# Decoder layer on one core: the 4-bit code lookup of the feed-forward takes its maxima with one four-way reduction for each side of the table

## Chip, core and metric

The kernel runs on one core of one Trainium2 chip. The metric is the device time of one execution, in microseconds (us). The core has five engines that run at the same time: TensorE (PE in the profile, with PEld for the loading of its weights), VectorE (DVE), ScalarE (ACT), GpSimd (POOL) and SyncE (SP), which here only issues DMA transfers. Each engine works through its own instructions in order and waits on semaphores for the others.

## The reference, cut to what matters

A decoder layer on x of 4 x 512 rows and 1024 columns: self-attention, cross-attention, and a feed-forward whose three weight matrices are stored as 4-bit codes with one scale for each block of 64.

```
NF4_CODE = [-1.0, -0.696, -0.525, -0.395, -0.284, -0.185, -0.091, 0.0, 0.080, 0.161, 0.246, 0.338, 0.441, 0.563, 0.723, 1.0]
Wg, Wu, Wd = NF4_CODE[codes] * scale of the block            # each 1024 x 3584 in all
g = x @ Wg.T ;  u = x @ Wu.T ;  h = silu(g) * u ;  x = x + h @ Wd.T
```

The table value of a code is computed without a gather. The table is convex above its zero and concave below. So the value is the maximum of four straight lines of the code (with a zero cut-off in one of them) less the maximum of four others. The change concerns how these two maxima are taken.

## The kernel before, in words

First comes the attention part (until about 946 us of the span), which the change doesn't touch. Then comes `feed_forward`. The hidden size of 3584 is cut into 28 chunks of 128, and two chunks make a group, so there are 14 groups. Group 0 and the last are written out, and those between are a hardware loop. On TensorE a group is `gate_up` for both chunks: eight steps q = 0 to 7, each with 24 gate and 24 up matmuls of 512 columns. Then follows `down`, with 16 row tiles r of 12 matmuls each, which sum into two PSUM buffers in turn. Down of row r waits for `y_added` of row r - 2. A gate or up matmul of step n waits until the PSUM bank of step n - 2 has been read (`silu_done`, `h_done`).

While TensorE works on a group, the other engines make the weights of the tiles to come: 12 tiles of 128 x 512 in a group, numbered k, six of them ahead of the group. For one tile:

- SP loads codes and scales into one of two slots (`codes`, `scales`).
- ACT draws eight lines of the codes (`draw_line`, L1547 for the first two, with Relu, and L1550 for the rest) into the tile `line`. There is one set of eight lines only, so a line is drawn anew when DVE has finished with the old one.
- DVE takes six pairwise maxima (`look_up`, L1625): upper and lower lines alternate, and each result overwrites the next line of its side. A seventh instruction, L1631, writes the difference into `w32` (two buffers).
- POOL multiplies by the scales (`scale`, L1426). ACT rounds to fp16 (`cut_high`, L1555, which comes after the third line of the tile two further on). POOL takes the remainder (`cut_low`, L1431), and `w_low` counts these.

DVE also does `hidden` for each step q (L1661, h = silu(g) * u, from PSUM) and `add_down` for each row r (L1666, adds into y). ACT does `gate_silu` (L1578) and `hidden_high` (L1583), POOL `hidden_low` (L1445). The order on each engine is written out by hand. `CUTS` says which of a group's 84 lookup instructions (7 for each of 12 tiles) DVE issues in which step q; the last 14 are interleaved with `add_down`, one after each row. `FIRST_CUTS` does so for group 0, in which the layer norm is done between the first steps. The lookups of step q come ahead of `hidden(q)`. ACT draws lines one tile ahead of DVE, by the same cuts; `gate_silu(q)` comes after three quarters of the lines of its step, and in the first two steps of group 0 the layer norm's ACT work comes behind them.

Of the kernel before, what the change touches and what calls it, by code (L numbers as in the profile page):

```python
# [8 lines left out]
FP32 = mybir.dt.float32  # L9
# [3 lines left out]
ALU = mybir.AluOpType  # L13
ACT = mybir.ActivationFunctionType
AX_X = mybir.AxisListType.X
# [6 lines left out]
P = 128  # L22
# [8 lines left out]
HALF = 512  # L31
# [17 lines left out]
def code_line(lo, hi):  # L49

    slope = np.float32(F_SCALE * (NF4[hi] - NF4[lo]) / (hi - lo))
    return float(slope), float(np.float32(F_SCALE * NF4[lo] - float(slope) * lo))
# [4 lines left out]
UPPER_LINES = [code_line(8, 9), code_line(10, 11), code_line(12, 13), code_line(14, 15)]  # L57
LOWER_LINES = [tuple(-v for v in code_line(*at)) for at in ((5, 6), (3, 4), (1, 2), (0, 1))]


LINES = [line for pair in zip(UPPER_LINES, LOWER_LINES) for line in pair]
NL = len(LINES)
LUT = 7


class Attention:
# [1187 lines left out]
def feed_forward(nc, dram):  # L1254

    with ExitStack() as ctx:
        def sb(name, shape, dt):
            return ctx.enter_context(nc.sbuf_tensor(name, shape, dt))
# [15 lines left out]
        dn_l = sb("dn_l", [P, 2, C], FP16)  # L1274
        codes = sb("codes", [P, 2, HALF], INT32)
        scales = sb("scales", [P, 2, HALF], FP32)
        line = sb("line", [P, NL, HALF], FP32)
        above = sb("above", [P, 1], FP32)
        below = sb("below", [P, 1], FP32)
        w32 = sb("w32", [P, 2, HALF], FP32)  # L1280
# [16 lines left out]
        consts = sem("consts")  # L1297
# [8 lines left out]
        lined = sem("lined")  # L1306
        lut = sem("lut")
        scaled = sem("scaled")
        w_high = sem("fw_high")
        w_low = sem("fw_low")  # L1310
# [14 lines left out]
        NQ = 2 * NB  # L1325
        AHEAD = 6
# [11 lines left out]
            return (2, (k - 6) // 2, k % 2) if k < 10 else (3, 0, k % 2)  # L1338


        CUTS = [0, 9, 18, 27, 36, 45, 54, 62, 70, 84]
        FIRST_CUTS = [-14, -7, 0, 7, 14, 28, 42, 56, 70, 84]

        def cuts_of(first):
            return FIRST_CUTS if first else CUTS


        def ended_in(q, first):
            lo, hi = cuts_of(first)[q:q + 2]
            return range(lo // LUT, hi // LUT)  # L1350

        def lines_in(q, first):
            lo, hi = cuts_of(first)[q:q + 2]
            return range(NL + lo * NL // LUT, NL + hi * NL // LUT)

# [3 lines left out]
        def last_k(last):  # L1359
            return 6 if last else PER  # L1360
# [46 lines left out]
        @block.gpsimd  # L1407
        def _(pool):
            nc.gpsimd.memset(ident[:, :], 0.0).then_inc(consts, 1)
            nc.gpsimd.memset(minus_half[:, :], -0.5).then_inc(consts, 1)  # L1410
            nc.gpsimd.memset(zero[:, :], 0.0).then_inc(consts, 1)
            nc.gpsimd.memset(above[:, :], LINES[0][1]).then_inc(consts, 1)
            nc.gpsimd.memset(below[:, :], LINES[1][1]).then_inc(consts, 1)
            pool.wait_ge(consts, 5)
            nc.gpsimd.affine_select(out=ident[:, :], in_=ident[:, :], compare_op=ALU.not_equal, fill=1.0, base=0,
                                    pattern=[[-1, P]], channel_multiplier=1).then_inc(consts, 1)

            def held(ge_sem, value):
                pool.wait_ge(ge_sem, value)
                pool.sem_inc(pool_tick, 1)  # L1420

            def scale(i, k):
                t, w = AHEAD + PER * i + k, w32[:, k % 2, :]
                held(scales_loaded[k % 2], 32 * (PER // 2 * i + (AHEAD + k) // 2 + 1))
                held(lut, LUT * (t + 1))
                nc.gpsimd.tensor_tensor(w, w, scales[:, k % 2, :], ALU.mult).then_inc(scaled, 1)  # L1426

            def cut_low(i, k):
                w_h, w_l = weights(*tile_of(k))
                held(w_high, AHEAD + PER * i + k + 1)  # L1430
                nc.gpsimd.tensor_tensor(w_l, w32[:, k % 2, :], w_h, ALU.subtract).then_inc(w_low, 1)  # L1431

            def ln_root(r):
                s = slice(r % SLOTS, r % SLOTS + 1)
                pool.wait_ge(ln_stat, 4 * r + 4)
                nc.gpsimd.tensor_tensor(rstd[:, s], var_eps[:, s], minus_half[:, :], ALU.pow).then_inc(ln_rstd, 1)
                nc.gpsimd.tensor_tensor(neg_mean[:, s], zero[:, :], mean_var[:, r % SLOTS, 0:1], ALU.subtract)\
                    .then_inc(ln_rstd, 1)
                pool.wait_ge(ln_rstd, 3 * r + 2)
                nc.gpsimd.tensor_tensor(shift[:, s], neg_mean[:, s], rstd[:, s], ALU.mult).then_inc(ln_rstd, 1)  # L1440

            def hidden_low(i, q):
                cols = slice(T * (q % NB), T * (q % NB) + T)
                held(h_high, NQ * i + q + 1)
                nc.gpsimd.tensor_tensor(hT_l[:, q // NB, cols], h32[:, q % 2, :], hT_h[:, q // NB, cols],  # L1445
                                        ALU.subtract).then_inc(h_low, 1)

            def group(i, last, first=False):
                for q in range(NQ + 1):
                    if q > 0:  # L1450
                        hidden_low(i, q - 1)
                    for k in ended_in(q, first):
                        if k < last_k(last):
                            scale(i, k)
                            if not rows_of_step(q, first):
                                cut_low(i, k)
                    for r in rows_of_step(q, first):
                        if r + LEAD < RT:
                            ln_root(r + LEAD)
                    if rows_of_step(q, first):  # L1460
                        for k in ended_in(q, first):
                            cut_low(i, k)

            pool.sem_inc(h_low, FREE)
            for k in range(-AHEAD, -2):
                scale(0, k)
                cut_low(0, k)
            for r in range(8 + LEAD):
                ln_root(r)
            group(0, False, True)  # L1470
            with pool.Fori(1, GROUPS - 1) as i:
                group(i, False)
            group(GROUPS - 1, True)
# [63 lines left out]
        def _(act):  # L1537
            def draw_line(i, at):
                k, m = at // NL, at % NL
                t, slot = AHEAD + PER * i + k, k % 2  # L1540
                if m == 0:
                    act.wait_ge(codes_loaded[slot], 16 * (PER // 2 * i + (AHEAD + k) // 2 + 1))
                if k > -AHEAD:
                    act.wait_ge(lut, LUT * (t - 1) + min(m + 1, LUT))
                slope, intercept = LINES[m]
                if m < 2:
                    op = nc.scalar.activation(line[:, m, :], codes[:, slot, :], ACT.Relu, scale=slope,  # L1547
                                              bias=(above if m == 0 else below)[:, :])
                else:
                    op = nc.scalar.activation(line[:, m, :], codes[:, slot, :], ACT.Copy, scale=slope, bias=intercept)  # L1550
                op.then_inc(lined, 1)

            def cut_high(i, k):
# [62 lines left out]
        def _(dve):  # L1616
            def look_up(i, ops):
                for at in ops:
                    k, n = at // LUT, at % LUT
                    t = AHEAD + PER * i + k  # L1620
                    if n < LUT - 1:
                        dve.wait_ge(lined, NL * t + n + 3)
                        if n >= 2:
                            dve.wait_ge(lut, LUT * t + n - 1)
                        nc.vector.tensor_tensor(line[:, n + 2, :], line[:, n, :], line[:, n + 2, :], ALU.max)\  # L1625
                            .then_inc(lut, 1)
                    else:
                        dve.wait_ge(lut, LUT * t + n)
                        if k >= 2 - AHEAD:
                            dve.wait_ge(w_low, t - 1)  # L1630
                        nc.vector.tensor_tensor(w32[:, k % 2, :], line[:, NL - 2, :], line[:, NL - 1, :], ALU.subtract)\  # L1631
                            .then_inc(lut, 1)

            def ln_stats(r):
                s = r % SLOTS
# [34 lines left out]
            def group(i, last, first=False):  # L1670
                cuts = cuts_of(first)
                for q in range(NQ):
                    look_up(i, range(cuts[q], min(cuts[q + 1], LUT * last_k(last))))
                    hidden(i, q)
                    ln_rows(rows_of_step(q, first))
                for r in range(RT):
                    add_down(i, r)
                    if cuts[NQ] + r < LUT * last_k(last) and r < cuts[NQ + 1] - cuts[NQ]:
                        look_up(i, range(cuts[NQ] + r, cuts[NQ] + r + 1))

            look_up(0, range(-LUT * AHEAD, -2 * LUT))
            for r in range(LEAD):
# [66 lines left out]
```

## Time and profile before

| | |
|---|---|
| median of 3 runs | 2796.19 us (2792.77 to 2798.71) |
| the profiled execution's own time | 2796.21 us |
| its span, first to last instruction | 2794.3 us |
| busy | PE 92%, DVE 74%, ACT 56%, POOL 44% |
| largest DVE group | L1625, 1008 instructions, 919.4 us |

The profile is one execution. For each engine it shows the busy time, for each group of instructions the mean duration, and for idle time what ended it. Idle time of an engine that isn't the bottleneck costs nothing.

### The profile page before, as it was taken

The page shows a single profiled execution, that of the slowest core. Times are in us where ns is not written, and L with a number is a line of the kernel's source. Part 1 is how long each engine was busy: PE and PEld are TensorE (multiplying, and loading weights), DVE is VectorE, ACT ScalarE, POOL GpSimd, SP SyncE. Part 2 cuts the span into 40 slices and gives each one's busy share as a digit, 9 for nine tenths or more (in the row PEclk, how much of TensorE's full clock was granted, in tenths as well). Part 3 has the DMA queues.
Part 4 walks back from the last instruction along what each step waited for, and adds up shares of the span by engine and source line. Part 5 has one row for each costly group of instructions (what it writes and reads, how often), then busy time and mean ns, then how long its engine had stood idle before and what let it go on. Part 6 is the DMA issues. An engine that isn't in the chain of part 4 may idle for free.

```text
span 2794.3 us, 52658 instructions
## 1 busy us (share of the span) xinstructions
PE 2581.9 (92%) x18536; PEld 1397.0 (50%) x18536; DVE 2054.9 (74%) x2844; ACT 1572.4 (56%) x2794; POOL 1235.5 (44%) x1068
## 2 busy tenths in 40 slices
PE   5889999999974359899999999999999999999999
PEld 3567767667663234344444444444444444444444
DVE  4656768767775768787787869788787868778773
ACT  3456666656663468474655647465564747465550
POOL 2356667767774424252433424243433425243330
PEclk9999999999987669999999999999999999999999
DMA  5243433333222321111111112121111212111112
GB/s 192 91 132 100 121 114 120 102 111 100 81 73 59 128 80 56 51 61 38 60 49 50 53 45 60 38 68 38 53 52 45 61 38 66 40 60 46 52 34 120
DMA packets 153268, 205.34 MB, mean 73 GB/s; under 512 B 34160, under 2 KB 85872, under 8 KB 153072
## 3 DMA queue, kind: packets, MB, share of 16 engines
q1 hardware_dynamic: 153072, 202.97, 23.0%
q8 instruction: 93, 1.52, 0.2%
q14 instruction: 103, 0.84, 0.1%
HBM read 157.16 MB, written 44.04 MB: 72 GB/s over the span
## 4 chain that ended last, share of the span: by engine, by line
PE 60%; DVE 2%; issue 1%; ACT 1%; DMA 1%; POOL 0%; SPq 0%; DVEq 0%; ACTq 0%; POOLq 0%
PE f_bank L1501 39%; PE f_down L1521 21%; DVE line L1625 1%; DMA codes<-in_codes 1%; DVE f_stats L1639 0%; DVE fT_l L1652 0%; ACT f_xn L1561 0%; ACT line L1550 0%; ACT fT_h L1569 0%; PE f_down L1483 0%; DVE w L1631 0%; ACT line L1547 0%; DVE h L1661 0%; DVE y L1666 0%; DVE f_mean_var L1642 0%
## 5 line engine op out<-in xcount | busy, mean ns | idle before, releaser
L1625 DVE TENSOR_TENSOR line<-line 128x512 f32<-128x512 f32 x1008 | 919.4, 962 | 46.7 <-issue 30.9
L1550 ACT ACTIVATE line<-codes 128x512 f32<-128x512 int32 x1008 | 591.2, 620 | 382.6 <-DVE line L1625 284.8
L1501 PE MATMUL f_bank<-fT_h,up_h 128*128 128x512 f16 x1792 | 680.2, 380 | 3.7 <-DVE fT_l L1652 2.4
L1501 PE MATMUL f_bank<-fT_l,up_h 128*128 128x512 f16 x1792 | 680.2, 380 | 0.0
L1501 PE MATMUL f_bank<-fT_h,up_l 128*128 128x512 f16 x1792 | 680.2, 380 | 0.0
L532 POOL TENSOR_TENSOR p_l<-p,p_h 128x512 f16<-128x512 f32 x320 | 369.9, 1164 | 243.0 <-ACT p_h L945 242.6
L1666 DVE SCALAR_TENSOR_TENSOR y<-f_down,y 128x1024 f32<-128x1024 f32 x224 | 274.2, 1224 | 190.7 <-PE f_down L1521 190.7
L1431 POOL TENSOR_TENSOR up_l<-w,up_h 128x512 f16<-128x512 f32 x112 | 145.8, 1301 | 529.2 <-ACT up_h L1555 529.2
L1426 POOL TENSOR_TENSOR w<-w,scales 128x512 f32<-128x512 f32 x168 | 263.8, 1570 | 227.7 <-DVE w L1631 227.7
L1115 DVE TENSOR_REDUCE block_max<-bank 128x4 f32<-128x512 f32 x320 | 218.8, 686 | 195.3 <-PE bank L704 193.0
L1521 PE MATMUL f_down<-dn_h,hT_h 128*128 128x512 f16 x896 | 340.6, 380 | 9.0 <-DVE y L1666 9.0
L937 ACT ACTIVATE p<-bank 128x512 f32<-128x512 f32 x320 | 190.9, 597 | 271.6 <-PE bank L733 269.7
L1521 PE MATMUL f_down<-dn_l,hT_h 128*128 128x512 f16 x896 | 340.6, 380 | 0.0
L1521 PE MATMUL f_down<-dn_h,hT_l 128*128 128x512 f16 x896 | 340.4, 380 | 0.0
L1501 PEld LDWEIGHTS f_bank<-fT_h,up_h 128*128 128x128 f16 x1792 | 175.5, 98 | 214.7 <-DVE fT_l L1652 2.8
L1501 PEld LDWEIGHTS f_bank<-fT_h,up_l 128*128 128x128 f16 x1792 | 175.5, 98 | 212.1 <-issue 1.1
L1501 PEld LDWEIGHTS f_bank<-fT_l,up_h 128*128 128x128 f16 x1792 | 175.5, 98 | 210.3 <-issue 0.6
L1445 POOL TENSOR_TENSOR hT_l<-h,hT_h 128x512 f16<-128x512 f32 x112 | 172.9, 1543 | 237.3 <-ACT hT_h L1583 237.3
L1547 ACT ACTIVATE line<-codes,above 128x512 f32<-128x512 int32 x168 | 119.9, 714 | 218.3 <-DVE line L1625 183.6
L674 PE MATMUL bank<-xT,w_h 128*128 128x512 f16 x720 | 220.2, 388 | 10.8 <-POOL vx_h L602 10.8
L1661 DVE SCALAR_TENSOR_TENSOR h<-f_bank,h 128x512 f32<-128x512 f32 x112 | 77.1, 688 | 164.5 <-PE f_bank L1501 156.6
L945 ACT ACTIVATE p_h<-p 128x512 f16<-128x512 f32 x320 | 192.0, 621 | 0.0
(157 smaller groups left out, 4245.4 us busy)
## 6 DMA issues: line engine op xcount, KB each, us to landing
codes<-in_codes SPq DMA_DIRECT2D x168, 256.0 KB, 3.0
scales<-in_scales SPq DMA_DIRECT2D x336, 128.0 KB, 2.9
nat_parts<-nat SPq DMA_DIRECT2D x48, 256.0 KB, 2.0
q_rows<-nat_parts SPq DMA_DIRECT2D x96, 128.0 KB, 2.7
x_unit<-in_x SPq DMA_DIRECT2D x64, 128.0 KB, 2.7
x<-x_unit SPq DMA_DIRECT2D x64, 128.0 KB, 2.3
y<-x SPq DMA_DIRECT2D x4, 2048.0 KB, 12.3
out<-y SPq DMA_DIRECT2D x16, 512.0 KB, 2.6
```

The source lines that it names most:

```text
L532: nc.gpsimd.tensor_tensor(p_l[:, n % 2, k, :], p32[:, f % 3, :], p_h[:, n % 2, k, :], ALU.subtract).then_inc(p_low, 1)
L674: mm = nc.tensor.matmul(dst[:, :], w[:, c, cols], xT[:, :, half, c, :], start=(c == 0 and m == 0), stop=(c == CT - 1 and m == 2))
L937: nc.scalar.activation(p32[:, f % 3, :], bank[T_BANK + T_OF[f % CHUNKS]][:, :], ACT.Exp, scale=SELF_SCALE).then_inc(t_exp, 1)
L945: nc.scalar.activation(p_h[:, n % 2, k, :], p32[:, f % 3, :], ACT.Copy).then_inc(p_high, 1)
L1115: nc.vector.reduce_max(block_max[:, n % PAIRS, k, :], bank[S_BANK + S_OF[k]][:, :].rearrange("p (a n) -> p a n", n=P), AX_X)\
L1426: nc.gpsimd.tensor_tensor(w, w, scales[:, k % 2, :], ALU.mult).then_inc(scaled, 1)
L1445: nc.gpsimd.tensor_tensor(hT_l[:, q // NB, cols], h32[:, q % 2, :], hT_h[:, q // NB, cols], ALU.subtract).then_inc(h_low, 1)
L1501: mm = nc.tensor.matmul(bank[(GATE, UP)[kind] + n % 2][:, :], w[:, chunk, kind, P * c:P * c + P], x[:, c, cols], start=(m == 0), stop=(m = ...
L1521: mm = nc.tensor.matmul(down_bank[r % 2][:, half, :], h[:, m // 3, rows], w[:, m // 3, cols], start=(m == 0), stop=(m == 5))
L1550: op = nc.scalar.activation(line[:, m, :], codes[:, slot, :], ACT.Copy, scale=slope, bias=intercept)
L1625: nc.vector.tensor_tensor(line[:, n + 2, :], line[:, n, :], line[:, n + 2, :], ALU.max)\
L1666: nc.vector.scalar_tensor_tensor(y[:, r, :], down_bank[r % 2][:, :, :].rearrange("p a n -> p (a n)"), 1.0 / (H_SCALE * F_SCALE), y[:, r, : ...
```

## The change

The lines of one side now lie side by side (`line` is [P, 2, 4, 512] in place of [P, 8, 512]), and ACT draws the four upper ones and then the four lower ones. DVE takes the maximum over the four lines of a side in one `reduce_max`. It reads them through a rearranged view in which the four lines are the innermost dimension, so that successive words are 2048 bytes apart. The upper maximum goes straight to `w32`, the lower one to a new tile `side`, and a third instruction subtracts. A tile so takes 3 DVE instructions in place of 7 (`LUT = 3`), and the cuts are rescaled. ACT waits once for each side, ahead of its first line, and DVE waits for all four lines of a side. The wait for `w_low` of the tile two before, which stood ahead of the last of the seven, stands ahead of the first of the three, since that is now the one that writes `w32`. In the down stage a lookup instruction comes after every second row.

```diff
-LINES = [line for pair in zip(UPPER_LINES, LOWER_LINES) for line in pair]
+LINES = UPPER_LINES + LOWER_LINES
 NL = len(LINES)
-LUT = 7
+LUT = 3
...
-        line = sb("line", [P, NL, HALF], FP32)
+        line = sb("line", [P, 2, NL // 2, HALF], FP32)
+        side = sb("side", [P, HALF], FP32)
...
-        CUTS = [0, 9, 18, 27, 36, 45, 54, 62, 70, 84]
-        FIRST_CUTS = [-14, -7, 0, 7, 14, 28, 42, 56, 70, 84]
+        CUTS = [0, 4, 8, 12, 15, 19, 23, 27, 30, 36]
+        FIRST_CUTS = [-6, -3, 0, 3, 6, 12, 18, 24, 30, 36]
...
                 if m == 0:
                     act.wait_ge(codes_loaded[slot], 16 * (PER // 2 * i + (AHEAD + k) // 2 + 1))
-                if k > -AHEAD:
-                    act.wait_ge(lut, LUT * (t - 1) + min(m + 1, LUT))
+                which, n = 2 * m // NL, m % (NL // 2)
+                if k > -AHEAD and n == 0:
+                    act.wait_ge(lut, LUT * (t - 1) + which + 1)
                 slope, intercept = LINES[m]
-                if m < 2:
-                    op = nc.scalar.activation(line[:, m, :], codes[:, slot, :], ACT.Relu, scale=slope,
-                                              bias=(above if m == 0 else below)[:, :])
+                out = line[:, which, n, :]
+                if n == 0:
+                    op = nc.scalar.activation(out, codes[:, slot, :], ACT.Relu, scale=slope,
+                                              bias=(above, below)[which][:, :])
...
-                    if n < LUT - 1:
-                        dve.wait_ge(lined, NL * t + n + 3)
-                        if n >= 2:
-                            dve.wait_ge(lut, LUT * t + n - 1)
-                        nc.vector.tensor_tensor(line[:, n + 2, :], line[:, n, :], line[:, n + 2, :], ALU.max)\
+                    w = w32[:, k % 2, :]
+                    if n < 2:
+                        dve.wait_ge(lined, NL * t + NL // 2 * (n + 1))
+                        if k > -AHEAD:
+                            dve.wait_ge(lut, LUT * t)
+                        if n == 0 and k >= 2 - AHEAD:
+                            dve.wait_ge(w_low, t - 1)
+                        nc.vector.reduce_max((w, side[:, :])[n], line[:, n, :, :].rearrange("p m n -> p n m"), AX_X)\
                             .then_inc(lut, 1)
                     else:
-                        dve.wait_ge(lut, LUT * t + n)
-                        if k >= 2 - AHEAD:
-                            dve.wait_ge(w_low, t - 1)
-                        nc.vector.tensor_tensor(w32[:, k % 2, :], line[:, NL - 2, :], line[:, NL - 1, :], ALU.subtract)\
-                            .then_inc(lut, 1)
+                        dve.wait_ge(lut, LUT * t + 2)
+                        nc.vector.tensor_tensor(w, w, side[:, :], ALU.subtract).then_inc(lut, 1)
...
                 for r in range(RT):
                     add_down(i, r)
-                    if cuts[NQ] + r < LUT * last_k(last) and r < cuts[NQ + 1] - cuts[NQ]:
-                        look_up(i, range(cuts[NQ] + r, cuts[NQ] + r + 1))
+                    if r % 2 == 0 and r // 2 < cuts[NQ + 1] - cuts[NQ]:
+                        n = cuts[NQ] + r // 2
+                        look_up(i, range(n, min(n + 1, LUT * last_k(last))))
```

## Rows read from the trace of the kernel before

**Rows 1.** Windows: start:end, length, busy (count) by engine, clock, DMA share, GB/s.
```profile
1126.00:1135.00 9.00, 0.11 (x1) 0.00 (x0) 8.97 (x10) 6.71 (x12) 6.16 (x5) 0.70 0.17 58
1135.00:1141.00 6.00, 5.87 (x17) 2.23 (x18) 3.19 (x5) 1.96 (x3) 0.00 (x0) 0.60 0.27 89
1141.00:2790.00 1649.00, 1649.00 (x7641) 747.35 (x7638) 1264.81 (x1387) 895.40 (x1567) 597.90 (x410) 1.00 0.16 52
```
**Rows 2.** Waits between 940 and 1170 us: total, times, longest.
```profile
PE f_down L1521 <- DVE y L1666: 9.0, 1, 9.0
```
**Rows 3.** Line L1625 alone: duration min/median/max in ns, first and last start.
```profile
L1625 DVE TENSOR_TENSOR line<-line x1008: 674/683/1766, 956.0 to 2711.2; 128x512 f32<-128x512 f32 x168
```
**Rows 4.** DVE reductions and a reciprocal, by form: count | busy us, mean ns.
```profile
L1115 DVE TENSOR_REDUCE block_max<-bank 128x4 f32<-128x512 f32 x320 | 218.8, 686 | 195.3 <-PE bank L704 193.0
L1125 DVE TENSOR_REDUCE row_max<-block_max 128x4 f32<-128x16 f32 x32 | 5.2, 161 | 0.1
L1159 DVE RECIPROCAL rx_sum<-bank 128x8 f32<-128x8 f32 x64 | 12.7, 198 | 6.0 <-PE bank L788 6.0
```
**Rows 5.** DVE in the loop, in time order: start us, us, instruction, idle before.
```profile
1225.76 0.69 DVE L1661 SCALAR_TENSOR_TENSOR h<-f_bank,h 128x512 f32<-128x512 f32 x1 [2.20 <-PE f_bank L1501]
1236.12 0.69 DVE L1661 SCALAR_TENSOR_TENSOR h<-f_bank,h 128x512 f32<-128x512 f32 x1 [1.91 <-PE f_bank L1501]
...
1259.36 1.22 DVE L1666 SCALAR_TENSOR_TENSOR y<-f_down,y 128x1024 f32<-128x1024 f32 x1 [1.83 <-PE f_down L1521]
1260.50 0.68 DVE L1625 TENSOR_TENSOR line<-line 128x512 f32<-128x512 f32 x1
1261.95 1.23 DVE L1666 SCALAR_TENSOR_TENSOR y<-f_down,y 128x1024 f32<-128x1024 f32 x1 [0.77 <-PE f_down L1521]
```
**Rows 6.** DVE in group 0, in time order: first lookups of steps 1 and 2, then steps 3 to 8.
```profile
1047.65 3.69 DVE L1625 TENSOR_TENSOR line<-line 128x512 f32<-128x512 f32 x6
...
1069.98 0.69 DVE L1661 SCALAR_TENSOR_TENSOR h<-f_bank,h 128x512 f32<-128x512 f32 x1 [1.84 <-ACT h L1578]
1070.58 4.47 DVE L1625 TENSOR_TENSOR line<-line 128x512 f32<-128x512 f32 x6
...
1078.09 0.69 DVE L1661 SCALAR_TENSOR_TENSOR h<-f_bank,h 128x512 f32<-128x512 f32 x1 [2.31 <-PE f_bank L1501]
1078.70 4.01 DVE L1625 TENSOR_TENSOR line<-line 128x512 f32<-128x512 f32 x6
...
1105.45 0.68 DVE L1661 SCALAR_TENSOR_TENSOR h<-f_bank,h 128x512 f32<-128x512 f32 x1
...
1119.37 0.68 DVE L1661 SCALAR_TENSOR_TENSOR h<-f_bank,h 128x512 f32<-128x512 f32 x1
...
1133.87 1.21 DVE L1666 SCALAR_TENSOR_TENSOR y<-f_down,y 128x1024 f32<-128x1024 f32 x1
```
**Rows 7.** ACT in group 0, steps 1 and 3, in time order.
```profile
1048.43 0.72 ACT L1547 ACTIVATE line<-codes,above 128x512 f32<-128x512 int32 x1 [2.79 <-DVE line L1625]
...
1072.13 0.72 ACT L1547 ACTIVATE line<-codes,above 128x512 f32<-128x512 int32 x1 [1.67 <-DVE line L1625]
1072.76 0.70 ACT L1547 ACTIVATE line<-codes,below 128x512 f32<-128x512 int32 x1
...
1077.01 0.57 ACT L1578 ACTIVATE h<-f_bank 128x512 f32<-128x512 f32 x1
1077.49 0.62 ACT L1550 ACTIVATE line<-codes 128x512 f32<-128x512 int32 x1
...
1082.59 2.69 ACT L1550 ACTIVATE line<-codes 128x512 f32<-128x512 int32 x5
```
**Rows 8.** POOL's cut_low line alone: duration min/median/max in ns.
```profile
L1431 POOL TENSOR_TENSOR up_l<-w,up_h x112: 1151/1314/1622, 963.6 to 2686.5; 128x512 f16<-128x512 f32 x112
```
**Rows 9.** The critical chain where group 0's first steps wait: start us, us, what.
```profile
1048.43 1.33 ACT line L1547 x2
...
1054.88 0.70 ACT f_xn L1561
```

More of the change, by code:

```diff
@@ L1412, in _ @@
             nc.gpsimd.memset(above[:, :], LINES[0][1]).then_inc(consts, 1)
-            nc.gpsimd.memset(below[:, :], LINES[1][1]).then_inc(consts, 1)
+            nc.gpsimd.memset(below[:, :], LINES[NL // 2][1]).then_inc(consts, 1)
             pool.wait_ge(consts, 5)
@@ L1542, in draw_line @@
                     act.wait_ge(codes_loaded[slot], 16 * (PER // 2 * i + (AHEAD + k) // 2 + 1))
-                if k > -AHEAD:
-                    act.wait_ge(lut, LUT * (t - 1) + min(m + 1, LUT))
+                which, n = 2 * m // NL, m % (NL // 2)
+                if k > -AHEAD and n == 0:
+                    act.wait_ge(lut, LUT * (t - 1) + which + 1)
                 slope, intercept = LINES[m]
-                if m < 2:
-                    op = nc.scalar.activation(line[:, m, :], codes[:, slot, :], ACT.Relu, scale=slope,
-                                              bias=(above if m == 0 else below)[:, :])
+                out = line[:, which, n, :]
+                if n == 0:
+                    op = nc.scalar.activation(out, codes[:, slot, :], ACT.Relu, scale=slope,
+                                              bias=(above, below)[which][:, :])
                 else:
-                    op = nc.scalar.activation(line[:, m, :], codes[:, slot, :], ACT.Copy, scale=slope, bias=intercept)
+                    op = nc.scalar.activation(out, codes[:, slot, :], ACT.Copy, scale=slope, bias=intercept)
                 op.then_inc(lined, 1)
```

## Prediction

> **What bounds the kernel now.** I read the windows first. From 1141 to 2790 us TensorE is busy for 1649.00 of 1649.00 us at a granted clock of 1.00, DVE for 1265, ACT for 895, POOL for 598 [rows 1]. So for thirteen of the fourteen groups TensorE alone sets the time, and a cheaper lookup there buys nothing: the share of 74% that DVE has on the page is no bound. The pace of the loop is in the DVE rows: `hidden` comes every 1236.12 - 1225.76 = 10.36 us, `add_down` every 2.59 us [rows 5], so a group is 8 x 10.36 + 16 x 2.59 = 124.3 us.
>
> Only group 0 has a place where the lookup decides. TensorE idles from 1126 to 1135 and then runs six microseconds at a mean clock of 0.60, between its two levels [rows 1]. It waits 9.0 us for `add_down` [rows 2], which stands behind the lookups of steps 4 to 7. These steps come every 1119.37 - 1105.45 = 13.92 us and not every 10.36 [rows 6]. Before them, in steps 0 and 1, ACT's first line waits for DVE, and layer-norm work waits behind ACT's lines on the critical chain [rows 9].
>
> **The price of the new instruction.** A reduction of 512 words takes 686 ns and one of 16 words in groups of four 161 ns [rows 4]. That is 525 / 496 = 1.06 ns per word and 144 ns fixed. For 2048 words: 0.144 + 2048 x 0.00106 = 2.31 us, if a word 2048 bytes from the last costs as much as its neighbour. A successor starts 0.08 us before an instruction ends (six maxima of 0.68 take 3.69 [rows 6]), so it occupies 2.23 us. The trace has no such reading. The reductions of rows 4 read runs of at least four words. The far end is the reciprocal of 8 words, 33 words apart in PSUM: 198 ns, so at most (198 - 144) / 8 = 6.8 ns per word, or 14 us for 2048. But that is another operation on another memory, and division may be all of it. I take the low end, since the reduction in groups of four is the same operation with the same output pattern, and keep dearer words as a rival. Nothing suggests less than one cycle per word.
>
> **The change part by part, in the loop.** Removed: 72 maxima per group at 0.60 (median 683 ns, up to 1766 [rows 3]). Added: 24 reductions x 2.23 = 53.5. With 12 differences and 8 `hidden` at 0.60 and 16 `add_down` at 1.14 [rows 5] DVE has 53.5 + 7.2 + 4.8 + 18.2 = 83.7 us of work in 124.3. The fullest step has three reductions, a difference and `hidden`: 7.9 of 10.36 us. In the down stage two rows now hold 1.14 + 2.23 + 1.14 = 4.5 of 5.18 us, so the second `add_down` still comes 0.7 us before TensorE needs the buffer. The gain in DVE time is hidden, and so is the coarser step.
>
> The finer waits also go. ACT draws a side only when the whole reduction of the tile before is done. DVE's first instruction of a tile waits for `w_low` of the tile two before; behind it on DVE stand `hidden` and `add_down`, for which TensorE waits. That `cut_low` follows ACT's `cut_high`, which follows the third line of the tile now drawn. So from the end of one upper reduction to the start of the next there are: 0.09 (1048.43 less the end of the first maximum [rows 6, 7]), a Relu line 0.63, two lines 1.04, `cut_high` 0.62, `cut_low` 1.15 at its shortest [rows 8], which it is when DVE no longer reads two SBUF tiles at once, and two hand-overs of 0.1: 3.7 us, or 4.2 with `hidden_high` between. A tile so takes at least 2.31 + 4.2 = 6.5 us. In the loop a tile has 8.3 us (10 tiles in 82.9), so this is covered by TensorE; in group 0's steps 4 to 7 it is not. The second tile of SBUF and two POOL memsets cost nothing; SP's order stays, its waits count whole tiles.
>
> **Group 0.** Steps 0 and 1: ACT's first line started 0.78 us after DVE's first instruction (1048.43 - 1047.65 [rows 6, 7]); now it starts 2.31 + 0.09 = 2.40 after. That is +1.6 us each on the critical chain, +3.2. Step 2 adds 1.6 in the same way, as its `hidden` is released by ACT. In step 3 DVE starts at 1070.58 + 1.6 = 1072.2, ACT's first line at 1074.6, `gate_silu` 1077.01 - 1072.13 = 4.9 later at 1079.5 for 0.57, `hidden` at 1080.2 and not 1078.09: +2.1 for both steps together. Steps 4 to 7, two tiles each, from DVE's start at 0: first upper reduction to 2.3, ACT's lines, `hidden_high` and `cut_high` to 5.2, `cut_low` to 6.5, second upper reduction 6.6 to 8.9; ACT's next upper lines and `cut_high` 9.0 to 11.7, one lower line, `gate_silu` to 12.9, `hidden` to 13.6. Four such steps are 54.4 where four took 1133.87 - 1078.70 = 55.2: -0.8. Sum: 3.2 + 2.1 - 0.8 = **+4.5 us** at the first `add_down`, and with it at TensorE's restart. The wait of 9.0 us is not cured: DVE gets shorter, but the loop over ACT and POOL takes its place. Against the profiled execution's own 2796.21 us (span 2794.3; the median is 2796.19): 2796.2 + 4.5 = **2800.7 us**.
>
> **The rivals.** *Dear words (slower).* Each word lies in a place of its own, and the read stream may not keep one per cycle. It decides in the down stage: a reduction that occupies more than 5.18 - 2 x 1.14 = 2.90 us, 1.38 ns per word or 1.3 times the row's, makes `add_down` late, and TensorE loses the excess four times in each of 13 groups. Midway between this onset and two cycles per word (4.40 us) lies 3.65: 13 x 4 x 0.75 = 39 us. In group 0 the upper three steps cost about 3.6 each and step 3 2.7 (ACT's lower lines wait until 7.4 us after DVE's start), steps 4 to 7 take 17.0, +12.8: +26. So 2796 + 65 = **2861 us**. *Two cycles per word.* DVE then has 20 x 4.4 + 10.8 = 98.8 us in the eight steps against 82.9, and 4 x 1.5 = 6.0 more in down: 22 x 13 = 286, and group 0 35: **3117 us**. For both speaks that the trace has no full-rate reading of scattered words; against them, that short groups cost nothing extra.
>
> The Trainium skill speaks against this change here. "Vector Engine (DVE) Microarchitecture Reference", section 5.2, "Measured stream behaviour on trn2", gives 1.73 ns per column when one source hops 4 KiB at every element, against 1.05 for adjacent pairs; by it the reduction would be an estimated 3.6 us and the sum near the first rival's. The same section reports one single-source stream that hopped 16 KiB at every element at full rate, which is my forecast's case. No row here tells which of the two holds at 2 KiB.
>
> *The stall goes (faster).* If ACT and POOL keep up better than reckoned, steps 4 to 7 run at TensorE's 10.36. Then the 9.0 us and the slow restart (6 us at 0.60, 2.4 lost [rows 1]) go, and the 3.2 stay: 2796.2 - 8.2 = **2788 us**. For it: DVE's own work in such a step is only 4 x 2.23 + 1.8 = 10.7 us. Against it: the wait for `w_low` that the change moves forward.
>
> **How the numbers follow.** Forecast (full rate, ACT and POOL loop) 0.48, its own range 2792 to 2812; dear words 0.28; two cycles or more 0.16; the stall goes 0.08. A measurement of this kernel tells about 0.2%, 5.6 us, from no change. Of the 0.48 I put 0.37 within 5.6 us, 0.08 above, 0.03 below. Faster 0.08 + 0.03 = 0.11, same 0.37, slower 0.28 + 0.16 + 0.08 = 0.52. The forecast is still the likeliest single case. The range goes from the fast rival, 2788, through the dear words to 3000; beyond it lie two cycles and more, which with little else make up the 2 in 10 left out.
>
> **What would show it.** The mean of the reduction: 2.3 us confirms the forecast, above 2.98 the rivals. TensorE's wait for y in group 0: still one of 8 to 11 us. ACT's first line 2.4 us behind DVE in steps 0 and 1. Steps 4 to 7 every 13.6 us. TensorE without idle after 1145. DVE's busy time should fall by about 919 - 336 x 2.31 = 143 us. I am wrong if the loop shows TensorE waiting for `add_down` in each group, or if the group 0 stall is gone.

## The result and the profile after

The changed kernel takes 2987.53 us (2984.44 to 2992.21) beside 2795.79 of the kernel before: ratio 1.0688, 95% interval 1.0672 to 1.0704, that is 188 to 197 us slower. The forecast of 2800.7 us is missed. The time lies inside the recorded range of 2788 to 3000 us, but only because that range is wide: none of the prediction's sums gives it. The dear-words rival gave 2861 us, so it holds in its cause and not in its size.

First the page of the changed kernel: busy time and share of each engine. Then its two reductions and TensorE's down matmuls from the groups (count | busy, mean ns | idle before, released by), and one row of the waits (total us, times, longest).

```profile
PE 2616.8 (88%) x18536; PEld 1399.2 (47%) x18536; DVE 2409.7 (81%) x2172; ACT 1549.9 (52%) x2794; POOL 1131.6 (38%) x1068
...
L1631 DVE TENSOR_REDUCE w<-line 128x512 f32<-128x2048 f32 x168 | 638.9, 3803 | 13.1 <-ACT line L1553 9.7
L1631 DVE TENSOR_REDUCE side<-line 128x512 f32<-128x2048 f32 x168 | 629.0, 3744 | 0.0
...
L1522 PE MATMUL f_down<-dn_h,hT_h 128*128 128x512 f16 x896 | 350.3, 391 | 143.1 <-DVE y L1669 143.1
```
```profile
PE f_down L1522 <- DVE y L1669: 143.1, 62, 21.6
```

A reduction takes 3.80 us and not 2.31: (3803 - 144) / 2048 = 1.79 ns per word, 1.7 times the row of the reductions of before [rows 4]. DVE's busy time rises by 355 us with a quarter fewer instructions. TensorE waits for `add_down` 62 times, where before it did once [rows 2].

The loop shows it. This window is one group of the changed kernel (columns as in rows 1), beside the third row of rows 1, where TensorE never idled.

```profile
1349.00:1486.00 137.00, 126.94 (x579) 56.44 (x577) 122.83 (x61) 69.00 (x124) 39.35 (x32) 0.98 0.15 46
```

Of the 12.6 us by which this window is longer than the 124.4 of a group before, TensorE idles 10.1, all of it for `add_down` (waits in the window, then the first matmul behind the longest of them):

```profile
PE f_down L1522 <- DVE y L1669: 10.1, 5, 7.5
...
1443.95 0.61 PE L1522 MATMUL f_down<-dn_h,hT_h 128*128 128x512 f16 x1 [7.53 <-DVE y L1669]
```

The other 2.5 us are matmuls that take longer. After the wait of 7.5 us the granted clock is 0.50, the lower of TensorE's two levels, from 1443.95 to 1446.95, and the matmuls take 0.61 to 0.63 us and not 0.38.

These are DVE's instructions in the group before that window, in time order (start us, us, instruction, idle before): two steps of the eight, then the start of the down stage.

```profile
1238.92 3.84 DVE L1631 TENSOR_REDUCE w<-line 128x512 f32<-128x2048 f32 x1
1242.66 3.78 DVE L1631 TENSOR_REDUCE side<-line 128x512 f32<-128x2048 f32 x1
1246.47 0.69 DVE L1635 TENSOR_TENSOR w<-w,side 128x512 f32<-128x512 f32 x1
1248.23 0.69 DVE L1664 SCALAR_TENSOR_TENSOR h<-f_bank,h 128x512 f32<-128x512 f32 x1 [1.06 <-ACT h L1581]
1248.84 3.78 DVE L1631 TENSOR_REDUCE w<-line 128x512 f32<-128x2048 f32 x1
1252.52 3.78 DVE L1631 TENSOR_REDUCE side<-line 128x512 f32<-128x2048 f32 x1
1256.33 1.01 DVE L1635 TENSOR_TENSOR w<-w,side 128x512 f32<-128x512 f32 x1
1258.61 0.69 DVE L1664 SCALAR_TENSOR_TENSOR h<-f_bank,h 128x512 f32<-128x512 f32 x1 [1.26 <-ACT h L1581]
...
1305.88 1.21 DVE L1669 SCALAR_TENSOR_TENSOR y<-f_down,y 128x1024 f32<-128x1024 f32 x1
1307.01 3.74 DVE L1631 TENSOR_REDUCE w<-line 128x512 f32<-128x2048 f32 x1
1310.66 2.35 DVE L1669 SCALAR_TENSOR_TENSOR y<-f_down,y 128x1024 f32<-128x1024 f32 x2
1312.92 3.74 DVE L1631 TENSOR_REDUCE side<-line 128x512 f32<-128x2048 f32 x1
1316.57 2.36 DVE L1669 SCALAR_TENSOR_TENSOR y<-f_down,y 128x1024 f32<-128x1024 f32 x2
```

Where `hidden` waits, it is no longer for TensorE, as in rows 5, but for ACT's `gate_silu`; this is so in four of the eight steps. In the down stage two rows take 1316.57 - 1310.66 = 5.91 us and not 5.18.

Where the 188.3 us of span come from can be read from the first `add_down` of each group. In group 0 it starts at 1169.13 and not 1133.87 [rows 6]: +35.3. (The attention part, which the change doesn't touch, ended 2.9 us earlier in this execution, at 943.44 and not 946.33 by the start of DVE's last instruction there. So the feed-forward up to there takes 225.7 us and not 187.5. The run words_alone below, with the same code to this point as the kernel before, took 190.5, so such a figure holds to about 3 us: the feed-forward is 35 to 38 us longer up to there.) The twelve groups to the last one take 2811.54 - 1169.13 = 1642.4 us, where twelve of 124.4 took 1493.0 before: +149.4, 12.4 a group. The rest of the last group, whose down stage still holds the three lookup instructions of one tile, adds the remaining 3.6.

### The profile page after: what moved, and what is told of

Read it like the earlier page. It is cut to its first block, busy times and chain, and to the rows that moved or that the text cites. A ratio compares the mean times of both kernels' runs of the same rounds, so it can differ in the third digit from the quotient of the medians.

```text
span 2982.6 us, 50330 instructions
## 1 busy us (share of the span) xinstructions
PE 2616.8 (88%) x18536; PEld 1399.2 (47%) x18536; DVE 2409.7 (81%) x2172; ACT 1549.9 (52%) x2794; POOL 1131.6 (38%) x1068
## 4 chain that ended last, share of the span: by engine, by line
DVE 25%; PE 22%; issue 16%; ACT 3%; DMA 1%; DVEq 1%; POOL 0%; SPq 0%; ACTq 0%; POOLq 0%
DVE side L1631 14%; PE f_bank L1502 11%; PE f_down L1522 10%; DVE w L1631 5%; DVE y L1669 3%; ACT line L1553 2%; DVE w L1635 1%; DMA codes<-in_codes 1%; ACT h L1581 1%; DVE h L1664 1%; DVE f_stats L1642 0%; DVE fT_l L1655 0%; ACT f_xn L1564 0%; ACT fT_h L1572 0%; ACT line L1550 0%
## 5 line engine op out<-in xcount | busy, mean ns | idle before, releaser
L1631 DVE TENSOR_REDUCE w<-line 128x512 f32<-128x2048 f32 x168 | 638.9, 3803 | 13.1 <-ACT line L1553 9.7
L1631 DVE TENSOR_REDUCE side<-line 128x512 f32<-128x2048 f32 x168 | 629.0, 3744 | 0.0
L1553 ACT ACTIVATE line<-codes 128x512 f32<-128x512 int32 x1008 | 583.7, 614 | 0.0
L1522 PE MATMUL f_down<-dn_h,hT_h 128*128 128x512 f16 x896 | 350.3, 391 | 143.1 <-DVE y L1669 143.1
L1432 POOL TENSOR_TENSOR up_l<-w,up_h 128x512 f16<-128x512 f32 x112 | 129.8, 1159 | 812.8 <-ACT up_h L1558 812.8
L1522 PE MATMUL f_down<-dn_l,hT_h 128*128 128x512 f16 x896 | 349.0, 390 | 0.0
L1522 PE MATMUL f_down<-dn_h,hT_l 128*128 128x512 f16 x896 | 347.8, 388 | 0.0
L1427 POOL TENSOR_TENSOR w<-w,scales 128x512 f32<-128x512 f32 x168 | 213.5, 1271 | 213.5 <-DVE w L1635 213.5
L1522 PEld LDWEIGHTS f_down<-dn_h,hT_h 128*128 128x128 f16 x896 | 89.4, 100 | 278.3 <-DVE y L1669 174.8
L1550 ACT ACTIVATE line<-codes,below 128x512 f32<-128x512 int32 x168 | 121.3, 722 | 163.6 <-DVE side L1631 163.6
```

Of the source, the lines that this page charges most:

```text
L1522: mm = nc.tensor.matmul(down_bank[r % 2][:, half, :], h[:, m // 3, rows], w[:, m // 3, cols], start=(m == 0), stop=(m == 5))
L1550: op = nc.scalar.activation(out, codes[:, slot, :], ACT.Relu, scale=slope, bias=(above, below)[which][:, :])
L1553: op = nc.scalar.activation(out, codes[:, slot, :], ACT.Copy, scale=slope, bias=intercept)
L1631: nc.vector.reduce_max((w, side[:, :])[n], line[:, n, :, :].rearrange("p m n -> p n m"), AX_X)\
```

## The experiments

**What the new instruction costs, alone.** `words_alone` is the kernel before, with measurements added behind its last store. The edit is shortened here: the loops that do each three times are left out, and so are six ACT lines behind them, three of 512 adjacent words (L1619) and three with words 16 bytes apart (L1621).

```diff
+            dve.wait_ge(stored, 16 * RT)
+            # three of each; y as one run of words, 2048 of them reduced by four to 512
+            reduce_max(out, flat[:, 0:2048].rearrange("p (n m) -> p n m", m=4), AX_X)              # L1708 adjacent fours
+            reduce_max(out, flat[:, 0:2048].rearrange("p (m n) -> p n m", m=4), AX_X)              # L1710 2048 bytes apart
+            reduce_max(out, y[:, 0:4, 0:512].rearrange("p m n -> p n m"), AX_X)                    # L1712 4 KiB
+            reduce_max(out, y[:, 0:16:4, 0:512].rearrange("p m n -> p n m"), AX_X)                 # L1714 16 KiB
+            reduce_max(out, flat[:, 0:2048].rearrange("p (b m n) -> p b n m", m=4, n=N), AX_X)     # L1716 N = 2 (8 bytes), L1718 4, L1720 32
+            reduce_max(out, flat[:, 0:1024].rearrange("p (m n) -> p n m", m=2), AX_X)              # L1722 two words, 2048 bytes apart
+            reduce_max(out, flat[:, 0:2048].rearrange("p (a n m) -> p n a m", a=2, m=2), AXES.XY)  # L1724 pair, hop, pair
+            tensor_tensor(out, ..., ALU.max)  # L1726 no input, L1728 one, L1730 both with words 16 bytes apart
```

> The kernel before, and behind its last store, when no other engine works, DVE reductions of 2048 words of y to 512 maxima, three of each: groups of four adjacent words; words 2048 bytes apart (as the change reads); 4 KiB apart; 16 KiB apart; 8, 16 and 128 bytes apart; two adjacent words and then a hop of 4 KiB; and two words 2048 bytes apart (1024 in all). Then pairwise maxima of 512 with none, one or both inputs 16 bytes apart, and ACT lines of 512 written side by side or 16 bytes apart. Theory 1, the place of successive words sets the price: fours of adjacent words take 0.144 + 2048 x 0.00106 = 2.3 us, words 2048 bytes apart 3.8 us as in the changed kernel. Rival A, a reduction that gives an output for every four words is itself that dear: both take 3.8 us. Rival B, other engines' traffic to the same memory made it dear: both take 2.3 us here. The kernel's own time grows by the tail that is added, about 120 us.

DVE in that stretch, by form (count | busy, mean ns):

```profile
L1718 DVE TENSOR_REDUCE f_xn<-y 128x512 f32<-128x2048 f32 x3 | 11.3, 3777 | 0.1
L1710 DVE TENSOR_REDUCE f_xn<-y 128x512 f32<-128x2048 f32 x3 | 11.2, 3733 | 0.1
L1712 DVE TENSOR_REDUCE f_xn<-y 128x512 f32<-128x2048 f32 x3 | 11.2, 3728 | 0.1
L1714 DVE TENSOR_REDUCE f_xn<-y 128x512 f32<-128x2048 f32 x3 | 11.2, 3727 | 0.1
L1720 DVE TENSOR_REDUCE f_xn<-y 128x512 f32<-128x2048 f32 x3 | 11.0, 3669 | 0.1
...
L1708 DVE TENSOR_REDUCE f_xn<-y 128x512 f32<-128x2048 f32 x3 | 6.9, 2286 | 2.7 <-DMA out<-y 2.7
L1716 DVE TENSOR_REDUCE f_xn<-y 128x512 f32<-128x2048 f32 x3 | 6.9, 2286 | 0.1
L1724 DVE TENSOR_REDUCE f_xn<-y 128x512 f32<-128x2048 f32 x3 | 6.9, 2286 | 0.1
L1722 DVE TENSOR_REDUCE f_xn<-y 128x512 f32<-128x1024 f32 x3 | 3.7, 1230 | 0.1
L1730 DVE TENSOR_TENSOR f_xn<-y 128x512 f32<-128x512 f32 x3 | 3.2, 1059 | 0.1
L1728 DVE TENSOR_TENSOR f_xn<-y 128x512 f32<-128x512 f32 x3 | 3.2, 1059 | 0.1
L1726 DVE TENSOR_TENSOR f_xn<-y 128x512 f32<-128x512 f32 x3 | 2.1, 691 | 0.1
```

Theory 1 holds and both rivals fall. Fours of adjacent words take 2.286 us, where the prediction's slope gave 2.31. With the words 2048 bytes apart it is 3.733 with nothing else running, so neither the groups of four nor the other engines make the price. The distance hardly matters from 16 bytes (3.78) to 16 KiB (3.73), while at 8 bytes the rate is full. ACT's lines, in time order:

```profile
2887.81 1.67 ACT L1619 ACTIVATE line<-y 128x512 f32<-128x512 f32 x3 [133.73 <-DVE f_xn L1730]
2889.39 2.88 ACT L1621 ACTIVATE line<-y 128x512 f32<-128x512 f32 x3
```

Taken one by one, a line takes 0.61 us with adjacent words and 1.08 to 1.10 with words 16 bytes apart. The whole kernel took 2894.32 us, one run, about 97 us more than the kernel before, where a tail of about 120 was expected.

**The same reductions over adjacent words.**

```diff
-        line = sb("line", [P, 2, NL // 2, HALF], FP32)
+        line = sb("line", [P, 2, HALF, NL // 2], FP32)
...
-                out = line[:, which, n, :]
+                out = line[:, which, :, n]
...
-                        nc.vector.reduce_max((w, side[:, :])[n], line[:, n, :, :].rearrange("p m n -> p n m"), AX_X)\
+                        nc.vector.reduce_max((w, side[:, :])[n], line[:, n, :, :], AX_X)\
```

> The changed kernel, but the four lines of a side are interleaved in SBUF: ACT writes each line at a step of 16 bytes, and DVE's reduction reads groups of four adjacent words. Order, waits and counts stay. Theory 1: the reductions take 2.3 us, the loop is bound by TensorE again, and the time is the recorded sum for full rate, about 2801 us, with TensorE still waiting some 10 us in group 0; if ACT's spread writes are dearer (up to 1.0 us a line and not 0.62), group 0 gets longer and the time is up to 2820. Rival A: the reductions stay at 3.8 us and the time at 2987.

Measured: 2983.68 us, ratio 1.0660 (1.0646 to 1.0675), a miss. The reductions cost 2.28 us as expected, yet the time is nearly that of the changed kernel. The price had moved to ACT, as its groups show:

```profile
L1553 ACT ACTIVATE line<-codes 128x512 f32<-128x512 int32 x1008 | 1076.2, 1152 | 0.0
L1550 ACT ACTIVATE line<-codes,above 128x512 f32<-128x512 int32 x168 | 206.4, 1228 | 385.9 <-DVE w L1631 367.2 <-DMA codes<-in_codes 18.5
```

A line written at a step of 16 bytes takes 1152 ns where it took 614 in the changed kernel. In the eight steps of the loop ACT is now nearly full: between 1219.11 and 1312.29 us it is busy for 89.3 of 93.2 us, DVE for 54.9. `gate_silu` stands behind these lines, and DVE's `hidden` waited for it 335 us in sum, beside 66 in the changed kernel. I had allowed 1.0 us a line and looked at group 0 only. That the time comes out so near that of the changed kernel is chance, since another engine sets it.

**The lower side first.** The edit against adjacent_fours:

```diff
-LINES = UPPER_LINES + LOWER_LINES
+LINES = LOWER_LINES + UPPER_LINES
...
-                        if n == 0 and k >= 2 - AHEAD:
+                        if n == 1 and k >= 2 - AHEAD:
                             dve.wait_ge(w_low, t - 1)
-                        nc.vector.reduce_max((w, side[:, :])[n], line[:, n, :, :], AX_X)\
+                        nc.vector.reduce_max((side[:, :], w)[n], line[:, n, :, :], AX_X)\
```

> As adjacent_fours, but the lower side is drawn and reduced first. Its maximum goes to the separate tile, so the wait for the cut_low of the tile two before stands ahead of the second instruction of the tile and not the first. Theory 2: that wait lengthens steps 4 to 7 of group 0 (by about 1 us each where ACT, POOL and DVE form a loop), so this is 3 to 5 us faster than adjacent_fours. Rival: the wait is met anyway, and the two are equal within 1 us.

Measured: 2984.88 us, ratio 1.0664 (1.0649 to 1.0678), equal to adjacent_fours. With ACT nearly full in the eight steps this says little about the wait, and the same edit stands again below.

**The coarser hand-over without the new instruction.**

```diff
-                        nc.vector.reduce_max((w, side[:, :])[n], line[:, n, :, :].rearrange("p m n -> p n m"), AX_X)\
-                            .then_inc(lut, 1)
+                        for m in range(1, NL // 2):
+                            if m > 1:
+                                dve.wait_ge(maxed_pair, 2 * (2 * t + n) + m - 1)
+                            out = line[:, n, m, :] if m < NL // 2 - 1 else (w, side[:, :])[n]
+                            nc.vector.tensor_tensor(out, line[:, n, m - 1, :], line[:, n, m, :], ALU.max)\
+                                .then_inc(maxed_pair if m < NL // 2 - 1 else lut, 1)
```

> The changed kernel's line order, cuts, waits of ACT and w_low wait, but each reduction is done as three pairwise maxima in a row, as the kernel before did them. It isolates the coarser hand-over from the new instruction. Theory 3: a side occupies DVE 3 x 0.6 = 1.8 us (more where POOL reads too), the loop stays bound by TensorE, and only group 0 changes: 2796 to 2804 us. Rival: the coarse hand-over itself stalls TensorE in every group, by several us: 2830 us or more.

Measured: 2823.88 us, ratio 1.0100 (1.0084 to 1.0115), 28 us slower by the ratio (23 to 32), between theory and rival and in neither. TensorE's waits for `add_down` from 1100 us on (total, times, longest):

```profile
PE f_down L1523 <- DVE y L1674: 26.2, 14, 11.9
```

The longest is in group 0; the other thirteen are 1.1 us each, about one a group, 14.3 us in sum. So the coarse hand-over with three maxima does stall TensorE along the loop, by about 1 us a group. The rest lies in group 0, where the first `add_down` comes 12 to 15 us later than before, counted from the end of the attention part. A step of group 0 shows what ends it (DVE, time order):

```profile
1125.79 0.69 DVE L1669 SCALAR_TENSOR_TENSOR h<-f_bank,h 128x512 f32<-128x512 f32 x1 [1.24 <-ACT h L1582]
...
1133.15 3.19 DVE L1636 TENSOR_TENSOR line<-line 128x512 f32<-128x512 f32 x2 [1.58 <-POOL up_l L1433]
...
1141.09 0.69 DVE L1669 SCALAR_TENSOR_TENSOR h<-f_bank,h 128x512 f32<-128x512 f32 x1 [1.24 <-ACT h L1582]
```

The step takes 15.3 us, where it took 13.9 before. DVE waits 1.58 us for POOL's `cut_low`, the wait that was moved forward, and 1.24 us for `gate_silu`. The pair of maxima that starts at 1133.15 takes 3.19 us and not 1.3; POOL works next to it until 1135.80.

**Both prices gone.** In words_alone the rate was full at 8 bytes, and for a pair, a hop and a pair.

```diff
-        line = sb("line", [P, 2, NL // 2, HALF], FP32)
+        line = sb("line", [P, 2, 2, HALF, 2], FP32)
...
-                out = line[:, which, n, :]
+                out = line[:, which, n // 2, :, n % 2]
...
-                        nc.vector.reduce_max((w, side[:, :])[n], line[:, n, :, :].rearrange("p m n -> p n m"), AX_X)\
+                        nc.vector.reduce_max((w, side[:, :])[n], line[:, n, :, :, :].rearrange("p a n m -> p n a m"),
+                                             AXES.XY)\
```

> The changed kernel, but the four lines of a side are stored as two pairs: the two lines of a pair alternate word by word, and the pairs lie 4 KiB apart. ACT writes each line at a step of 8 bytes, and DVE's reduction reads two adjacent words, hops, and reads two more, a form that took 2.286 us alone in words_alone, as reading at a step of 8 bytes did. At 16 bytes ACT's lines took 1.15 us and bound adjacent_fours. Theory: at 8 bytes ACT writes at its full rate, 0.62 us a line, and with both prices gone the order and the waits of the change are left alone: 2801 us by the recorded sum, 2805 to 2825 if the coarse hand-over costs what coarse_pairs showed (26 us). Rival: ACT at 8 bytes is as slow as at 16: 2984 us again.

Measured: 2806.6 us, ratio 1.0025 (1.0016 to 1.0034), that is 4.5 to 9.5 us slower than before. The reductions take 2.28 us and ACT's lines 0.66. DVE in group 0, then two windows:

```profile
1109.94 0.69 DVE L1666 SCALAR_TENSOR_TENSOR h<-f_bank,h 128x512 f32<-128x512 f32 x1 [1.25 <-ACT h L1582]
...
1117.28 2.29 DVE L1632 TENSOR_REDUCE w<-line 128x512 f32<-128x2048 f32 x1 [1.53 <-POOL dn_l L1433]
...
1123.75 0.69 DVE L1666 SCALAR_TENSOR_TENSOR h<-f_bank,h 128x512 f32<-128x512 f32 x1 [1.27 <-ACT h L1582]
```
```profile
1130.00:1139.00 9.00, 2.31 (x11) 0.87 (x9) 6.68 (x5) 7.99 (x15) 5.85 (x5) 0.93 0.17 58
...
1150.00:2790.00 1640.00, 1640.00 (x7600) 743.47 (x7598) 1114.70 (x776) 896.36 (x1562) 495.59 (x408) 1.00 0.17 52
```

The step takes 13.8 us (13.6 by the prediction), TensorE's wait for `add_down` in group 0 is 7.1 us (8 to 11 by the prediction), and the loop never stalls. This is the world of the forecast, whose sum was +4.5 us. Counted from the end of the attention part, the first `add_down` comes 6.5 us later than in the kernel before, 3.6 later than in words_alone.

**The wait that was moved forward, again.** The same edit as in adjacent_fours_lower_first, on adjacent_pairs.

> As adjacent_pairs, but the lower side is drawn and reduced first, so that the wait for the cut_low of the tile two before stands ahead of the second instruction of a tile. In adjacent_fours_lower_first the same edit showed nothing, but there ACT was the bound. In adjacent_pairs the second tile of each of steps 4 to 7 in group 0 waits 1.5 us for POOL at its first reduction, and such a step takes 13.8 us. Theory: the wait that the change moved forward costs this; with it later the steps take 12.3 to 13 us, and the time is 3 to 6 us below adjacent_pairs, a ratio to the kernel before of about 1.001. Rival: ACT's own work (gate_silu behind the lines) ends last in such a step anyway, the steps stay at 13.6 to 13.8 us and the ratio at 1.0025.

Measured: 2801.15 us, ratio 1.0012 (0.9998 to 1.0025). A step of group 0 takes 12.9 us:

```profile
1129.21 0.69 DVE L1666 SCALAR_TENSOR_TENSOR h<-f_bank,h 128x512 f32<-128x512 f32 x1 [1.13 <-ACT h L1582]
...
1135.69 2.29 DVE L1632 TENSOR_REDUCE side<-line 128x512 f32<-128x2048 f32 x1 [0.68 <-ACT line L1554]
...
1142.13 0.69 DVE L1666 SCALAR_TENSOR_TENSOR h<-f_bank,h 128x512 f32<-128x512 f32 x1 [1.14 <-ACT h L1582]
```

The wait for POOL is gone and a shorter one for ACT's line stands in its place. Steps 5 to 7 get 0.9 us shorter each. But step 4 takes 15.1 us and not 14.4, and steps 1 and 2 are about 0.5 us longer, so from TensorE's first work on the normed rows to the first `add_down` this execution gains only 0.7 us on that of adjacent_pairs. The two ratios point the same way but their intervals overlap. So the steps show that the wait costs 0.9 us in three of them; that the kernel gets faster without it is not shown.

**Why dear words cost 188 us and not 65.**

```diff
-                        if n == 3 * len(lines) // 4 and q < NQ:
+                        if n == (3 * len(lines) // 4 if first else 2) and q < NQ:
                             gate_silu(i, q)
```

> The changed kernel with gate_silu moved ahead on ACT in groups 1 to 13: behind the third line of its step and not behind three quarters of them. In the changed kernel hidden waits 1.1 to 1.3 us for gate_silu in four of eight steps of a group, because gate_silu stands behind lower lines which wait for DVE's reduction. Theory: these 4.6 us a group go, 13 x 4.6 = 60 us, to about 2927 us. Rival: DVE is full without them, and the time stays within 10 us of 2987.

Measured: 2938.34 us, ratio 1.0500 (1.0484 to 1.0515) beside 1.0688: 49 us less by the medians, 53 by the ratios, where 60 were expected and none by the rival. `hidden` now follows the difference at once:

```profile
1244.68 0.69 DVE L1635 TENSOR_TENSOR w<-w,side 128x512 f32<-128x512 f32 x1
1245.29 0.68 DVE L1664 SCALAR_TENSOR_TENSOR h<-f_bank,h 128x512 f32<-128x512 f32 x1
```

TensorE's waits for `add_down` fall from 143.1 to 96.0 us in sum. So about 4 of the 12.4 us a group came from `hidden`'s waits for `gate_silu`. The nearly full DVE waits for ACT's `gate_silu`, which stands behind lines that wait for DVE's reduction.

**A version that beats both.** The lookup of before had one stall, in group 0. To remove it takes no new instruction: `down` of group 0 needs the tiles up to k = 5, and those from k = 6 on are first used by the next group, so some of their lookups can move into the down stage.

```diff
-        FIRST_CUTS = [-14, -7, 0, 7, 14, 28, 42, 56, 70, 84]
+        FIRST_CUTS = [-14, -7, 0, 7, 14, 25, 36, 47, 58, 84]
...
-                    if cuts[NQ] + r < LUT * last_k(last) and r < cuts[NQ + 1] - cuts[NQ]:
-                        look_up(i, range(cuts[NQ] + r, cuts[NQ] + r + 1))
+                    if r < 14:
+                        lo, count = cuts[NQ], cuts[NQ + 1] - cuts[NQ]
+                        look_up(i, range(lo + count * r // 14, min(lo + count * (r + 1) // 14, LUT * last_k(last))))
```

> The kernel before, with nothing of the change: only FIRST_CUTS of group 0 is altered, so that steps 4 to 7 hold 11 lookups each and not 14, and the down stage takes the 26 that are left, up to two behind each of 14 rows. Theory: steps 4 to 7 fall from 13.9 to about 11 us, the wait of 9.0 us and the slow restart go, about 11 us: 2785 us. Rival: the lookups that are moved make add_down late in the down stage and give it back: 2796 us.

Measured: 2786.82 us, ratio 0.9957 (0.9945 to 0.9969), 12 us faster than the kernel before. The nine microseconds in which TensorE idled [rows 1] are full, at full clock:

```profile
1126.00:1135.00 9.00, 9.00 (x44) 4.05 (x43) 8.96 (x12) 5.42 (x9) 3.08 (x3) 1.00 0.16 58
1140.00:2775.00 1635.00, 1635.00 (x7577) 741.12 (x7575) 1262.47 (x1383) 896.46 (x1569) 597.37 (x410) 1.00 0.17 53
```

## Why the prediction was right or wrong, point by point

**The bound of the kernel before: right.** TensorE alone set the loop, and the lookup mattered in group 0 only. later_cuts gained 12 us, about the 11 of that stall and its slow restart, without touching the lookup's cost, and in adjacent_pairs a DVE that is busy for about 140 us less per 1640 bought nothing.

**The price of the reduction: the step that failed.** The forecast put a reduction at 2.31 us; it took 3.80. The prediction took the low end, "since the reduction in groups of four is the same operation with the same output pattern". Those rows read runs of four adjacent words, and words_alone shows that just this makes the difference: 2.286 us for adjacent fours, 3.733 for words 2048 bytes apart. The operation and its output were the same in both. The row spoke for its own read pattern, and none of before had the new one. Of the two figures in the Trainium skill ("Vector Engine (DVE) Microarchitecture Reference", section 5.2, "Measured stream behaviour on trn2") the first was the one that applied: 1.73 ns for a hop at every element, beside 1.75 alone and 1.79 in the kernel here. The prediction took the second for the forecast's case, but that stream alternates between two regions. It has its like here, two words 2048 bytes apart, 1.230 us for 1024. Four places in turn don't.

**Everything else in the forecast: right within its grain.** adjacent_pairs has the change's order and waits at the full rate, and comes out 4.5 to 9.5 us above the kernel before; the sum was +4.5. Its steps of 13.8 us and its full loop are the ones foretold; its stall of 7.1 us is a little below the 8 to 11. That the wait for `w_low` bites in group 0 is seen in coarse_pairs (1.6 us) and adjacent_pairs (1.5 us) and in three shorter steps of pairs_lower_first. That the coarser step costs nothing in the loop holds at 2.28 us a reduction; with three maxima in its place TensorE lost about 1.1 us a group.

**The dear-words rival: right in cause, wrong in size and in the main place.** It had TensorE lose 3.0 us a group, all within the down stage. Two rows of the down stage take 5.91 us, as 2 x 1.14 + 3.65 = 5.93 says. That 3.65 was right is luck: it was the middle between two bounds, and no row had it. Whether 2.90 us is the onset was not tried. But of the 10.1 us of waits in a group 7.5 come at the first row of the down stage, where DVE arrives late from the eight steps, and 2.6 in the rest.

The term that was mis-sized is the eight steps, which the rival left out as if TensorE's 82.9 us covered them. The prediction's own sum for two cycles, 20 reductions and 10.8, gives 83.8 us at 3.65, which is already more. They take 1305.88 - 1212.78 = 93.1. Of the excess of 9.3 over these 83.8 us, 4.6 are four waits for `gate_silu` (1.06, 1.26, 1.06 and 1.19 us), which early_silu shows. About 2.0 are reductions that follow each other every 3.70 to 3.80 us and not 3.65. The remaining 2.6 lie at the differences, which occupy up to 1.0 us and not 0.60; that POOL does this is only argued, though it is idle beside the one at 1246.47 (0.69 us) and works beside the one at 1256.33 (1.01 us). The prediction had worked out this same loop over ACT for group 0, and left it out of the loop stage, where it had TensorE as cover. At 3.65 us a reduction that cover was used up.

Group 0 was nearer: 35 to 38 us from the end of the attention part to the first `add_down`, where 26 was reckoned. Steps 4 to 7 take 18.0 us each and not 17.0. And 4 to 6 us of it lie ahead of all steps, in a part that no sum of the prediction has: DVE's lookups of the four tiles ahead of the layer norm take 32.5 us and not 23.8, and TensorE's first work on the normed rows starts 58.1 us after the end of the attention part, and not 51.8 (54.0 in words_alone).

**Two cycles per word** and **the stall goes** did not come. 1.79 ns is 1.7 times the 1.06 of the rows, and the stall of group 0 grew to 21.6 us.

## What to carry to other kernels

Take the price of an instruction from a row with the same read and write pattern, innermost step included. Where none is there, measure it behind the kernel's last store before anything is built on it. A layout that makes one engine's words adjacent can make another's scattered, as in adjacent_fours; look for a step that both take at full rate. And where an engine comes within a few per cent of the bound, count the waits in its chain with the others, since what hid them is gone.

## What the runs showed of the hardware

- A DVE reduction reads fp32 words at 1.05 ns a word when they are adjacent or 8 bytes apart, or in adjacent pairs with hops of 4 KiB between. At steps of 16 and 128 bytes and of 2, 4 and 16 KiB over four places it is 1.72 to 1.77 ns. Two places in turn, 2048 bytes apart, go at full rate (1.230 us for 1024 words). Why two do and four don't was not settled.
- A pairwise maximum of 512 takes 1059 ns with words 16 bytes apart in one input, and just the same in both, beside 691.
- ACT's write has the same edge: 0.62 us for a line of adjacent words, 0.66 at 8 bytes, 1.15 at 16 (1.10 with no other engine at work).
- After 7.5 us without work TensorE ran for 3.0 us at a granted clock of 0.50, in the changed kernel's loop.
